# Two LayerNorm halves moved from the feed-forward block into the two attentions

## The reference

```python
x = x + tanh(g_xattn[0]) * L0_xattn(layernorm(x), ctx)   # 16 heads of 96, 4 key heads
x = x + tanh(g_ffn[0])   * L0_ffn(layernorm(x))          # x@W.T + b + softmax-gated low-rank part
x = x + tanh(g_xattn[1]) * L1_xattn(layernorm(x), ctx)   # 32 heads of 128, 8 key heads, q and k RMS-normed
x = x + tanh(g_ffn[1])   * L1_ffn(layernorm(x))          # mixed streams, 50 Sinkhorn iterations

def layernorm(x, eps=1e-05):
    return (x - mean(x, -1)) / sqrt(var(x, -1) + eps)
```

## Time and profile before

| | |
|---|---|
| median of 3 runs | 2628.84 us (2624.82 to 2633.49) |
| the profiled execution | 2625.69 us, span of its trace 2623.9 us |
| PE busy, share of the span | 2405.3 us, 92% |
| DVE | 1481.2 us, 56% |
| ACT | 1075.4 us, 41% |
| POOL | 995.0 us, 38% |

### The profile page before, as it was taken

One profiled execution on the slowest core, in us unless ns is written; L12 is line 12 of the kernel. 1 busy time (PEld: TensorE's weight loads), 2 busy tenths in 40 slices (PEclk: granted clock), 3 DMA queues, 4 the chain that ended last, 5 costly groups with the idle time before them and its releaser, 6 DMA issues. The chain is left out here.

```text
span 2623.9 us, 34763 instructions
## 1 busy us (share of the span) xinstructions
PE 2405.3 (92%) x13032; PEld 2210.6 (84%) x13032; DVE 1481.2 (56%) x2352; ACT 1075.4 (41%) x2444; POOL 995.0 (38%) x812
## 2 busy tenths in 40 slices
PE   8999999979998899999879689999999999999724
PEld 6888888768998789998769578999999999999713
DVE  6222222132300566776677557777777777777797
ACT  3221222122311466667431245555555555554413
POOL 3000000000000446565253167667677677665110
PEclk9999999989999899999989899999999999999757
DMA  6222222143323223222213123333333333322001
GB/s 204 68 66 69 73 69 69 49 168 105 113 83 90 69 71 92 88 90 69 88 60 104 56 72 93 104 101 99 106 99 97 109 98 99 109 85 82 6 0 50
DMA packets 161240, 224.35 MB, mean 86 GB/s; under 512 B 31718, under 2 KB 124290, under 8 KB 160050
## 3 DMA queue, kind: packets, MB, share of 16 engines
q1 hardware_dynamic: 161074, 222.14, 27.2%
HBM read 183.81 MB, written 38.29 MB: 85 GB/s over the span
## 5 line engine op out<-in xcount | busy, mean ns | idle before, releaser
L967 POOL TENSOR_TENSOR attend_w_hi<-attend_w_raw,attend_one 128x1024 fp32r<-128x1024 f32 (+1 forms) x178 | 333.3, 1872 | 155.9 <-DMA attend_w_raw<-in_wo 81.5
L1146 DVE TENSOR_TENSOR attend_w_lo<-attend_w_raw,attend_w_hi 128x1024 fp32r<-128x1024 f32 (+1 forms) x184 | 252.4, 1372 | 206.3 <-ACT attend_w_hi L1034 123.1
L1284 PE MATMUL attend_ps_gemm<-normed_hi,attend_w_hi 128*128 128x400 f32 x704 | 246.5, 350 | 28.9 <-DVE attend_w_lo L1146 28.9
L1050 ACT ACTIVATE attend_p<-attend_p,attend_neg_max 100x361 f32<-100x361 f32 x256 | 150.9, 591 | 258.2 <-DVE attend_neg_max L1185 258.2
L1284 PE MATMUL attend_ps_gemm<-attend_o_hi,attend_w_hi 128*128 128x400 f32 x704 | 250.1, 355 | 4.4 <-issue 4.4
L1284 PE MATMUL attend_ps_gemm<-normed_lo,attend_w_hi 128*128 128x400 f32 x704 | 244.3, 347 | 0.0
L1284 PE MATMUL attend_ps_gemm<-normed_hi,attend_w_lo 128*128 128x400 f32 x704 | 243.5, 346 | 0.0
L1284 PE MATMUL attend_ps_gemm<-attend_o_hi,attend_w_lo 128*128 128x400 f32 x704 | 243.2, 346 | 0.0
L1284 PE MATMUL attend_ps_gemm<-attend_o_lo,attend_w_hi 128*128 128x400 f32 x704 | 243.2, 345 | 0.0
L301 DVE TENSOR_TENSOR context_k_square<-context_k_rows 128x512 f32<-128x512 f32 (+1 forms) x46 | 31.8, 691 | 346.7 <-ACT context_k_rows L226 346.6
L1059 ACT ACTIVATE attend_p<-attend_p,attend_exp_inv 100x361 f32<-100x361 f32 (+1 forms) x384 | 207.7, 620 | 0.0
(11 more groups left out here) (281 smaller groups left out, 6384.9 us busy)
## 6 DMA issues: line engine op xcount, KB each, us to landing
attend_w_raw<-in_wq SPq DMA_DIRECT2D x88, 512.0 KB, 4.0
attend_w_raw<-in_wo SPq DMA_DIRECT2D x64, 512.0 KB, 4.1
middle_w_raw<-in_wf SPq DMA_DIRECT2D x26, 512.0 KB, 3.5
attend_w_raw<-in_wo SPq DMA_DIRECT2D x32, 384.0 KB, 3.6
context_ctx_raw<-in_ctxT SPq DMA_DIRECT2D x8, 1456.0 KB, 7.2
attend_k_raw<-scratch_k SPq DMA_DIRECT2D x64, 180.5 KB, 3.6
context_ctx_raw<-in_ctxF SPq DMA_DIRECT2D x22, 512.0 KB
scratch_v<-context_v_out SPq DMA_DIRECT2D x44, 256.0 KB, 2.2
```

What stands on the lines that cost most here:

```text
L967: pool.tensor_tensor(hi, w_flat(w_raw, j % RAW, j), one[:hi.shape[0]].to_broadcast(hi.shape), ALU.mult).then_inc(w_hi_done, 1)
L1050: act.activation(p[:, slot, h], p[:, slot, h], ACT.Exp, bias=neg_max[:, slot, h:h + 1], accum_out=exp_sum[:, slot, h:h + 1]).then_inc(expe ...
L1146: dve.tensor_tensor(w_flat(w_lo, j % SPLIT, j), w_flat(w_raw, j % RAW, j), w_flat(w_hi, j % SPLIT, j).bitcast(F32), ALU.subtract).then_inc ...
L1284: mm = pe.matmul(out, left[a](c), right[b](c), start=(c == 0 and a == b == 0), stop=(c == chunks - 1 and a == 1))
```

## The change

Norm 0 goes into `attend` of layer 0, norm 3 into `attend` of layer 1; norms 1 and 2 stay in `middle` and are renumbered 0 and 1. In `attend`, tables say at which unit each step stands, always at the end of that unit's list on its engine:

| step | engine | layer 0, at unit | layer 1, at unit |
|---|---|---|---|
| `add_tokens` (4) | POOL | 20, 20, 21, 21 | 1, 2, 3, 4 |
| mean: matmul, then copy | PE, ACT | 22 | 5 |
| `centre` (4) | DVE | 23, 23, 24, 24 | 6, 7, 8, 9 |
| `square_centred` (4) | ACT | 24, 24, 25, 25 | 7, 8, 9, 10 |
| `add_squares` (3), `fold_squares` | POOL | 25, 26, 26, 26 | 9, 10, 11, 12 |
| variance: matmul, then root | PE, ACT | 27 | 13 |
| `invert_root` | DVE | 28 | 14 |
| `scale` (4; each centres again, then multiplies) | DVE | 28, 29, 29, 30 | 15, 16, 17, 18 |
| `round_normed` (4) | ACT | 29, 30, 30, 31 | 16, 17, 18, 19 |
| `remainder_normed` (4) | DVE | 30, 31, 31, 31 | 17, 18, 19, 20 |

The sums over chunks are made on POOL, so that one matmul does for each reduction. The two matmuls use `ps_gemm`'s banks in the line of the others. In `attend` of layer 1 the first query of the second half waits for the new `ln_lo`. `gate_in` goes, and the program's DMA scratch is given a size of 1024.

```diff
@@ attend
+    PAIRS = NC // 2
+    if layer == 0:
+        NORM_HALF, C_SLOTS = 0, 4
+        ADD_AT, MEAN_AT, CENTRE_AT, ... = (20, 20, 21, 21), 22, (23, 23, 24, 24), ...
+    else:
+        NORM_HALF, C_SLOTS = 1, 3
...
@@ POOL
+            def add_squares(k):
+                pool.wait_ge(norm_squared, k + 1)
+                if k > 1:
+                    pool.wait_ge(norm_added, PAIRS + k - 1)
+                pool.tensor_tensor(norm_sum[:], norm_sum[:], centred[:, k % C_SLOTS], ALU.add).then_inc(norm_added, 1)
...
@@ ACT
+            def root_variance():
+                at = gemm_at["var", 0, 0]
+                act.wait_ge(gemm_done, at + 1)
+                act.activation(norm_rstd[:], ps_gemm[:, at % 2, :HT], ACT.Sqrt, bias=norm_eps[:]).then_inc(norm_rooted, 1)
...
@@ DVE
+            def centre(n):
+                k = n % PAIRS
...
+                dve.tensor_tensor(centred[:, k % C_SLOTS], norm_pair(tokens, k),
+                                  norm_mean[:].unsqueeze(1).to_broadcast([P, 2, HT]), ALU.subtract).then_inc(centred_done, 1)
+            def scale(k):
+                centre(PAIRS + k)
+                dve.wait_ge(centred_done, PAIRS + k + 1)
+                dve.tensor_tensor(centred[:, k % C_SLOTS], centred[:, k % C_SLOTS],
+                                  norm_rstd[:].unsqueeze(1).to_broadcast([P, 2, HT]), ALU.mult).then_inc(norm_scaled, 1)
...
@@ DVE, end of a unit
                 remainder_q(query_of(u))
+                for m in range(PAIRS):
+                    if u == CENTRE_AT[m]:
+                        centre(m)
+                if u == INVERT_AT:
+                    invert_root()
+                for m in range(PAIRS):
+                    if u == LOW_AT[m]:
+                        remainder_normed(m)
+                    if u == SCALE_AT[m]:
+                        scale(m)
@@ middle, POOL
-            pool.wait_ge(ln_lo_done, PAIRS)
             for j in range(EARLY, EARLY + 3):
                 weights(j)
             add_bias(0)
@@ middle, PE
             pe.wait_ge(consts, CONSTS)
-            for c in range(NC):
-                mean_part(0, c)
-            mean(1)
-            variance_parts(0)
             for s in range(2):
                 for t in range(TILES):
                     product(s, t)
                     if s == 1 and t == 0:
                         extra(0, NC - 1)
-                    if s == 1 and t == 2:
-                        mean(2)
-                    if t == (3 if s == 0 else 7):
-                        variance(s + 1)
+                    if t == 1 + s:
+                        mean(s)
                     if t == QK:
                         score(s)
-                    if t == QK + 1:
+                    if t == QK + 2:
                         turn(s)
-                    if t > QK + 1:
+                    if t == QK + 3:
+                        extra(s, 0)
+                        extra(s, 1)
+                    if t > QK + 3:
                         extra(s, t - QK - 2)
-                    if s == 1 and t >= QK + 4:
-                        pe.wait_ge(o_read, NC + t - QK - 3)
-                        mean_part(3, t - QK - 4)
+                    if t == QK + 4:
+                        variance(s)
             extra(1, NC - 1)
-            for c in range(TILES - QK - 4, NC):
-                pe.wait_ge(o_read, NC + c + 1)
-                mean_part(3, c)
-            variance_parts(3)
```

More of the change, by code:

```diff
@@ L842, in attend @@
         place = {tile: j for j, tile in enumerate(tiles)}
-        gemms = [(kind, n, half) for kind, n in tiles for half in range(2 if kind == "o" else 1)]
+        gemms = [("q", n, 0) for n in range(LEAD)]
+        for u in range(NU + 1):
+            for v in (range(NU - HB, NU) if u == NU else range(max(u - HB, 0), max(u - HB + 1, 0))):
+                gemms += [("o", v, 0), ("o", v, 1)]
+            if u < NU and query_of(u) is not None:
+                gemms.append(("q", query_of(u), 0))
+            if u == MEAN_AT:
+                gemms.append(("mean", 0, 0))
+            if u == VAR_AT:
+                gemms.append(("var", 0, 0))
         gemm_at = {gemm: j for j, gemm in enumerate(gemms)}
@@ L1026, in _ @@
                 squares(query_of(u))
+                for k in range(PAIRS):
+                    if u == ADD_AT[k]:
+                        add_tokens(k)
+                    if k and u == GATHER_AT[k - 1]:
+                        add_squares(k)
+                if u == FOLD_AT:
+                    fold_squares()
         @block.scalar
@@ L1030, in _ @@
             act.wait_ge(side_load, 16 * (1 + layer))
[L1031 removed]
+            act.activation(gate[:], gate[:], ACT.Tanh).then_inc(gated, 1)
             for j in range(SPLIT):
@@ L1293, in queries @@
                 pe.wait_ge(w_lo_done, j + 1)
+                if layer == 1 and n == G * QT:
+                    pe.wait_ge(ln_lo_done, PAIRS)
                 bank_free(at)
@@ L1308, in outputs, with norm_gemm @@
                         (lambda h: o_hi[:, i % 2, h], lambda h: o_lo[:, i % 2, h]))
+            def norm_gemm(kind):
+                at = gemm_at[kind, 0, 0]
+                pe.wait_ge(norm_added, PAIRS if kind == "mean" else 2 * PAIRS)
+                bank_free(at)
+                pe.matmul(ps_gemm[:, at % 2, :HT], mean_w[:], norm_sum[:, 0], start=True, stop=True).then_inc(gemm_done, 1)
             def sum_squares(n):
@@ new lines, in _ @@
+            multiply_k(0, 1)
+            dve.wait_ge(bm_hi_done, 1)
+            dve.tensor_tensor(bm_lo[:], bm_raw[:], bm_hi[:].bitcast(F32), ALU.subtract).then_inc(bm_lo_done, 1)
+            split(6)
+            maxima(0)
+            gating(0)
+            split(7)
+            weigh(0)
+            sum_squares(0)
+            split(8)
+            accumulate(0, 0)
+            split(9)
+            accumulate(0, 1)
+            invert(0)
+            split(10)
+            accumulate(0, 2)
@@ new lines, in _ @@
+            normalise(0, 0)
+            normalise(0, 1)
+            split(11)
+            accumulate(0, 3)
+            normalise(0, 2)
+            normalise(0, 3)
+            split(12)
+            for m in range(4, NC):
+                if m < 6:
+                    remainder(0, 2 * m - 8)
+                    remainder(0, 2 * m - 7)
+                accumulate(0, m)
+                split(9 + m)
+            dve.wait_ge(o_read, NC)
+            sum_tokens(1)
+            multiply_k(1, 0)
@@ L1814, in _ @@
-            for k in range(PAIRS):
-                centre(3, k)
-            invert(3)
-            for k in range(PAIRS):
-                normalise(3, k)
-            for k in range(PAIRS):
-                remainder(3, k)
+            split(25)
+            for m in range(4, NC):
+                accumulate(1, m)
+                remainder(1, m - 4)
         @block.tensor
```

254 lines of the change are left out of this document (134 added, 120 removed).

## The result

The changed kernel takes 2646.2 us (median of 4 runs, 2644.55 to 2647.65) against 2628.4 (4 runs, 2624.82 to 2633.49): a ratio of 1.0066, 95% interval 1.0048 to 1.0084. It is slower by 0.7%, 18 us, where no change was forecast; the time lies inside the range (2603 to 2647), less than 1 us from its upper end, and it does so only because the range was drawn past the centre of the slower rival.

What follows compares the result with a forecast made beforehand. PE, 92% busy, bounds the kernel, so a step counts only where PE stops or has less to do. Middle -43.4, layer 0's attention +23.3, layer 1's +20.9 sum to +0.8 us; forecast 2628 us, range 2603 to 2647.

Steps and rivals of the forecast that it cites:

- slower rival: Layer 1's attention: POOL and DVE hold each other up, costing 35.5 us there; total 2645 us, chance 0.24.
- start of the middle: Middle: norm 0 no longer stands ahead of product(0, 0), which moves from 1328.07 to about 1307.8; -20.2 us.
- the end: End of middle: one remainder is left after the last accumulate, so the next block starts 20.4 us earlier.
- two new waits on w_lo: Middle, tile 8 of both halves: PE waits about 2.4 us for w_lo; with what follows, 4.6 per half, +9.2.
- the ring: Layer 0's late units: DVE and ACT's loop o_hi, o_lo, pt_lo, maxima, exponentials sets the pace; added DVE work costs full time.
- about half of its 1.7 us is hidden in the ring: Layer 0's attention: the lower clock after each PE gap costs 1.7 us, half hidden; 4 us for five gaps.
- the bound (28): Layer 0's attention: upper bound of 28 us on the forecast +23.3, with each centre doubled by POOL.
- Unit 27: Layer 0: variance matmul 0.2 and root 1.0 us; the skill's table-switch rule would add some 1.4 us.
- two passes (15, 16) 0.6 each; three (17, 18) 1.5 each: Layer 1's attention: us lost in units with two or three DVE passes, within 7 us for all passes.
- PE's own two matmuls: Layer 1's attention, where PE is full: the mean and variance matmuls cost 1.5 us.
- The faster one: Rival: the work hides in POOL's and DVE's idle time in layer 1, costing 6.5 there; 2605 us, chance 0.31.
- leads of 0.6 and 1.6 us: Layer 1's attention: how early v_lo (0.6) and pt_lo (1.6) are ready before PE wants them, around 1708.

Runs made afterwards that it cites:

- short additions: Changed kernel with seven of each attention's eight GpSimd additions cut to 8 columns in place of 400: 2630.7 us, 1.0011 to the kernel before.
- passes moved: Changed kernel with VectorE's norm passes moved into its idle time (layer 0 before the o_hi wait, layer 1 between o_lo and q_lo): 2612.6 us.
- additions moved: Changed kernel with GpSimd's additions ahead of the splitting of the query's squares, no longer behind it: 2633.1 us, 1.0020 to the kernel before.
- passes spread: Changed kernel with passes and additions moved, at most three passes per layer 0 unit, sums of squares behind tile 8's split: 2593.9 us.
- last tile behind the last unit: Kernel with the passes spread, but layer 0's last-tile centring, scaling, rounding and two remainders behind the last unit, among the accumulates: 2592.0 us.
- gaps of layer 0 filled as well: Changed kernel with short additions plus 10, 30, 26 and 20 extra products in TensorE's four layer 0 gaps: 2618.3 us, 0.9953.
- together with the passes: Changed kernel with both moves, VectorE's passes in its idle time and GpSimd's additions ahead of the squares: 2598.6 us, 0.9882.

## Why the prediction was wrong

The two attentions were put at 44.2 us and cost 58.5. These 14.3 us are most of the 18 that the forecast was off; the rest are the 1.4 us ahead of unit 20 and the 1.9 us in the last block, which no instruction of the change explains.

**What bounds the kernel, and the middle: right.** From layer 0's last matmul to layer 1's first product the trace lost 43.2 us; 43.4 were forecast. The start of the middle gave -20.7 (-20.2). Block start to last accumulate, which holds that, went from 170.0 to 146.8, -23.2 (-23.0), and the end gave -20.5 (-20.4). Inside, the two new waits on w_lo were 2.53 and 1.22 (2.4 each with more behind), and a wait of 2.56 for the second mean, behind a sum of tokens that POOL drew out, was not foreseen; the sum held because the errors cancelled, which is luck.

**Layer 0's attention: the mechanism right, two sizes wrong.** That each pass at the end of a unit costs its time in the ring is what the trace shows; the passes with the small matmuls were put at 19.3 us and measure 20.9 with the other two effects taken out. The step that failed is "about half of its 1.7 us is hidden in the ring, and I take 4 for five gaps". None of it was hidden: four gaps cost 7.4 us net, 1.7 to 3.2 each, at most 0.5 of it by a longer pass. The second is that the doubling of a centre beside POOL stood only in the bound (28): the two centres of unit 24 took 4.10 us, and short additions gave 4.0 back. 20.9 + 7.4 + 4.0 is 32.3, against the 31.3 measured. Unit 27, where the prediction weighed a longer change of function table, grew by 0.8 against 1.2 forecast: the load took 1.28 us, and the root began 1.30 behind its start.

**Layer 1's attention: the passes undersized, the additions about right.** POOL's additions were put at 10.4. Their waits are 10.0 us; moving them gave 13.3 in the changed kernel and 10.1 (14.8 to 4.6) in the one with the passes moved, and the granted clock of units 0 to 4 is 0.91 in the changed kernel, 0.97 with the additions moved, and 0.91 and 0.92 in the other pair. So the term is 10 to 13 us and what it has above the waits goes with the clock. DVE's passes were put at 7, and 2 for the clock; moving them gave 12.4. The steps that failed are "two passes (15, 16) 0.6 each; three (17, 18) 1.5 each" and the reciprocal's 0.6: they cost 1.1 and 1.5, 4.0 and 3.3, and the reciprocal 1.6 (2.3 with the variance matmul, which stays at 0.7 when the passes are moved). I had taken a pass at 0.93 us against a lead of 1.6 us; three passes beside square_lo and w_hi of POOL take 5.4 (0.98, 1.84, 2.56). PE's own two matmuls, 1.5, are right: with the passes moved, the offset grows by 0.7 behind each.

**The rivals.** The faster one is refuted by the offsets of all three stretches. The slower one had the time (2645) and its mechanism for layer 1, 16 for the passes and 14 for POOL's additions where 12.4 and 10.1 to 13.3 came; but it had 26 for layer 0, which came to 31.3, and 35.5 for layer 1, which came to 27.2. Its errors cancelled in part, so its number was partly luck. My mistake in weighing it was to let the leads of 0.6 and 1.6 us speak against it: they were read from units without the added work, and where POOL and DVE draw each other out a pass is longer than the 0.93 us set against the lead.

**What stays open.** Layer 1's attention costs 1.8 us in the kernel with the passes spread and 4.4 in the one with the last tile behind the last unit, and 19.2 with short additions and 14.8 with the gaps of layer 0 filled as well, though each pair issues the same instructions there. All but 1.4 us of the second difference, and all of the first, arise in the first five units, and the traces show the granted clock beside it: over units 0 to 4 it is 0.97 with the passes spread and 0.92 with the last tile moved, and 0.93 and 0.95 in the other pair. The additions moved alone and together with the passes, whose instructions are the same in these units too, cost 0.0 and 2.9 us there at 0.97 and 0.92. One place where it parts is the wait at `weigh_values`. PE in the kernel with the passes spread, its first matmul after the wait and the 7 us from there:
```profile
1558.64 0.42 PE L1513 MATMUL attend_ps_out<-attend_pt_hi,attend_v_hi 121*128 121x400 f32 x1 [2.73 <-issue]
1558.60:1565.60 7.00, 6.96 (x42) 1.00 0.37 101
```
The same in the kernel with the last tile behind the last unit:
```profile
1555.29 0.67 PE L1517 MATMUL attend_ps_out<-attend_pt_hi,attend_v_hi 121*128 121x400 f32 x1 [2.71 <-issue]
1555.20:1562.20 7.00, 6.91 (x23) 0.57 0.32 101
```
After 2.73 us idle the clock stayed at 2.4 GHz; after 2.71 it stood at 1.2 for most of the stretch. In the kernel before it fell after the same gap of 2.71, but only behind the first matmul, which still took 0.42. What decides it wasn't tried. The remaining cost of the middle's second mean wasn't either.

## What to carry to other kernels

Where a block of extra work has to go, its place in the unit matters more than its amount: the same work cost 58.5 us with its passes and additions at the end of the units and 16.8 where their engines stood idle, and those gaps were readable in the trace before (2.53 us ahead of o_lo in most late units of layer 0, about 2.4 between o_lo and q_lo in layer 1). Price a two-input VectorE pass by what GpSimd does at that moment, not by its length when alone; and count a gap of TensorE of 4 us or more, as the four here were, twice: once as the wait and once as the slow stretch behind it. A gap of 2.5 to 3 us had that stretch behind it in some of these kernels and not in others, so compare single prices of a few us only beside the granted clock of both traces. When the gains of a change come out to the microsecond and the total doesn't, take the added work out altogether first: one run told that the whole loss in the attentions was in it.

## What the runs showed of the hardware

- Adding 102 matmuls to idle stretches of TensorE shortened these stretches by 7.4 us: their granted clock went from 0.73 to 0.81 up to 1.00. The kernel's time fell by 12 us (2646.2 to 2633.8), but what the two traces show of the rest arose where nothing was changed.
- A gap of 2.71 to 2.73 us was followed by a granted clock of 1.00 over 7 us in one kernel and 0.57 in another with the same instructions there; over layer 1's first units that pair differs by 2.7 us.
- An addition on GpSimd of 128 x 16 elements took 0.20 to 0.23 us ten times out of fourteen, and 0.99 where it met a centre; one of 128 x 800 mostly took 1.9.
- Beside GpSimd a VectorE pass of 0.98 us took up to 2.56, and GpSimd's own 1.9 became 2.64: the two draw each other out, not only one of them.
